# When the expert weights, the residual rows and the empty rows are loaded beside the attention of a cross-attention and mixture-of-experts kernel, and how far the weighted sums follow the scores

## What is computed

```
c = layernorm(x); q = ctx
s = (c*w_cq) @ q.T + (c @ w_c + b_c)[:, None] + (q @ w_q + b_q)[None, :] + b_cq
a = softmax(s, axis=1);  c2q = a @ q
b = softmax(max(s, axis=1));  q2c = b @ c
x = x + concat([c, c2q, c*c2q, c*q2c]) @ W_l.T + b_l
y = layernorm(x);  e = argmax(y @ wr + br)        # one of 8 experts per row
x = x + gelu(y @ w1[e] + b1[e]) @ w2[e] + b2[e]   # w1: 8 x 128 x 512, w2: 8 x 512 x 128
```

## Time and profile before

| what | us |
|---|---|
| median of 3 runs (lowest, highest) | 244.3 (244.2, 244.76) |
| the profiled execution | 246.33 |
| its span | 244.6 |
| TensorE busy | 199.7 (82%) |
| VectorE busy | 182.6 (75%) |
| ScalarE busy | 157.6 (64%) |
| GpSimd busy | 124.0 (51%) |
| DMA, hardware queue | 50.08 MB, 89.6% of 16 engines' span |

### The profile page before, as it was taken

The page is one execution under the profiler, slowest core; times in us unless marked ns, Lnnn a source line. Parts: engine busy times, 40 slices in busy tenths (PEclk is TensorE's granted clock), DMA queues, the critical chain, the costliest instruction groups (busy, mean ns, idle before and its releaser), DMA issues.

```text
span 244.6 us, 4979 instructions
## 1 busy us (share of the span) xinstructions
PE 199.7 (82%) x1833; PEld 149.1 (61%) x1833; DVE 182.6 (75%) x400; ACT 157.6 (64%) x248; POOL 124.0 (51%) x171
## 2 busy tenths in 40 slices
PE   0388849875749999999999999989995589799980
PEld 0133344652436776677676776769974479689960
DVE  2899865786229989899999799886886437577670
ACT  2732795684346996969979969689701437467640
POOL 3792414700597094299780997942400650016783
PEclk9999986999988999999999999999998579999995
DMA  6999998999999999999999999998950159999100
GB/s 225 381 200 232 221 214 189 198 247 244 225 219 240 209 268 272 203 226 205 242 197 271 230 208 219 194 233 185 191 123 3 65 202 345 325 382 365 47 22 0
DMA packets 141102, 51.78 MB, mean 212 GB/s; under 512 B 121108, under 2 KB 138917, under 8 KB 141078
## 3 DMA queue, kind: packets, MB, share of 16 engines
q1 hardware_dynamic: 140144, 50.08, 89.6%
q0 software_dynamic: 784, 1.38, 1.6%
q10 hardware_dynamic: 150, 0.00, 0.0%
HBM read 10.74 MB, written 3.75 MB: 59 GB/s over the span
## 4 chain that ended last, share of the span: by engine, by line
PE 36%; DMA 15%; SPq 13%; DVE 11%; issue 11%; POOL 7%; ACT 4%; POOLq 0%; DVEq 0%; ACTq 0%
SPq L383 9%; DMA PT<-Phl 7%; PE psX L1032 7%; PE psS L1016 5%; PE psS L1014 5%; PE psS L1015 5%; PE psO L1032 5%; POOL out_x L568 4%; DMA stageT<-in_ctxT 4%; PE psX L1034 4%; DVE Phl L782 3%; POOL rows_by_expert L562 3%; DMA S<-rows_by_expert 3%; PE psO L1034 2%; ACT S L618 2%
## 5 line engine op out<-in xcount | busy, mean ns | idle before, releaser
L765 DVE TENSOR_SCALAR_CACHE_REDUCE S<-psS 128x1024 f32<-128x1024 f32 x48 | 58.3, 1217 | 11.9 <-PE psS L1016 11.7
L618 ACT ACTIVATE S<-S,negb 128x1024 f32<-128x1024 f32 x48 | 55.0, 1145 | 15.5 <-DVE negb L773 15.5
L782 DVE TENSOR_TENSOR Phl<-S,Phl 128x1024 f16<-128x1024 f32 x39 | 51.7, 1325 | 15.3 <-ACT Phl L633 15.2
L633 ACT CAST Phl<-S 128x1024 f16<-128x1024 f32 x48 | 50.2, 1045 | 16.4 <-DMA PT<-Phl 15.1
L500 POOL TENSOR_TENSOR Phl<-S,Phl 128x256 f16<-128x256 f32 x36 | 23.5, 685 | 53.2 <-ACT Phl L633 53.2
L1032 PE MATMUL psO<-qn,PT 128*128 128x256 f16 x204 | 36.5, 273 | 6.6 <-DMA PT<-Phl 6.6
L1014 PE MATMUL psS<-qT,gh 128*128 128x512 f16 x96 | 38.3, 399 | 3.1 <-DVE gl L743 2.8
L1032 PE MATMUL psX<-qn,PT 128*128 128x256 f16 x204 | 37.6, 279 | 3.7 <-DMA PT<-Phl 3.7
L1015 PE MATMUL psS<-qT,gh 128*128 128x512 f16 x96 | 37.9, 395 | 0.0
L1016 PE MATMUL psS<-qT,gl 128*128 128x512 f16 x96 | 37.9, 395 | 0.0
L1034 PE MATMUL psX<-qn,PT 128*128 128x128 f16 x204 | 36.2, 223 | 0.0
(11 more groups left out here) (232 smaller groups left out, 421.6 us busy)
## 6 DMA issues: line engine op xcount, KB each, us to landing
PT<-wp SPq DMA_DIRECT2D x8, 512.0 KB, 7.4
stageT<-in_ctxT SPq DMA_DIRECT2D x6, 512.0 KB, 7.2
qn<-wp SPq DMA_DIRECT2D x6, 512.0 KB, 8.5
wp<-in_w SPq DMA_DIRECT2D x4, 512.0 KB, 4.8
stageT<-in_w SPq DMA_DIRECT2D x4, 512.0 KB, 4.7
rows_by_expert<-stageT SPq DMA_DIRECT2D x4, 385.5 KB, 4.3
S<-rows_by_expert SPq DMA_DIRECT2D x2, 514.0 KB, 7.5
S<-rows_by_expert SPq DMA_DIRECT2D x2, 385.5 KB, 7.1
```

Source lines behind the costliest of these rows:

```text
L618: nc.scalar.activation(slot(t, e), slot(t, e), ACT.Exp, bias=negb[:, t:t + 1], accum_out=Lp[:, t * NG + e:t * NG + e + 1]).then_inc(exp_do ...
L633: nc.scalar.copy(hi, slot(t, e)).then_inc(high_done, 1)
L765: nc.vector.tensor_scalar(out=into, in0=bank(u, n)[:, 0:into.shape[1]], scalar1=1.0 / GS, scalar2=None, op0=ALU.mult, op1=ALU.max, accum_o ...
L782: nc.vector.tensor_tensor(lo, slot(t, e), hi, ALU.subtract).then_inc(low_done, 1)
```

## The change

On SP: the qn transposes are issued in the order 0, 2, 1, 3, 5, 4, 6, with no load between them. Two w1 loads follow them, ahead of PT(0,0); the other two come behind PT(1,0) and PT(1,3). The w2 loads come behind PT(t,5) of tiles 1 to 4, x_re behind PT(2,2), and the five fills behind PT(7,6). On GpSimd: product, cast and gl of the late columns of c, the first two of which were ScalarE's. On ScalarE: the copies of cT come before the first exp. On TensorE: `turn_c(1)` ahead of S(0,6), `row_terms()` ahead of S(1,5), and W(0,0..3) behind S(1,3..6), W(0,4..6) behind S(2,0..2); from W(1,0) on as before. The rest of GpSimd's program is unchanged.

```diff
@@ -372,8 +372,7 @@
             sp.dma_start(wrs[:, :], wr).then_inc(late_landed, 16)
             sp.dma_start(wl[:, :, :], wlT.rearrange("(k p) o -> p k o", p=P)).then_inc(late_landed, 16)
 
-            k = E // H
-            for n in range(NG):
+            for n in (0, 2, 1, 3, 5, 4, 6):
                 sp.wait_ge(qTh_ready, n + 1)
                 if n in DVE_LOW:
                     sp.wait_ge(qTl_ready, DVE_LOW.index(n) + 1)
@@ -381,9 +380,6 @@
                     sp.wait_ge(qTl_pool_ready, POOL_LOW.index(n) + 1)
                 src, dst = rows_of(n)
                 sp.dma_start_transpose(dst, src).then_inc(qn_landed[n], 16)
-                if n < H:
-                    sp.dma_start(w1raw[:, n * WC:(n + 1) * WC].rearrange("p (e f) -> p e f", f=F),
-                                 w1[n * k:(n + 1) * k].rearrange("e h f -> h e f")).then_inc(w_landed[n], 16)
 
             def transpose(t, e):
 
@@ -393,31 +389,42 @@
                 src, _, _, dst = piece(t, e)
                 sp.dma_start_transpose(dst, src).then_inc(pT_landed[e], 16)
 
+            def load_w1(k):
+
+                n = E // H
+                sp.dma_start(w1raw[:, k * WC:(k + 1) * WC].rearrange("p (e f) -> p e f", f=F),
+                             w1[k * n:(k + 1) * n].rearrange("e h f -> h e f")).then_inc(w_landed[k], 16)
+
             def load_w2(k):
 
                 n = E // H
                 sp.dma_start(stageT[:, k * WC:(k + 1) * WC].rearrange("p (e k d) -> p e k d", k=FC, d=D),
                              w2[k * n:(k + 1) * n].rearrange("e (k p) d -> p e k d", p=P)).then_inc(w_landed[H + k], 16)
 
+            load_w1(0)
+            load_w1(1)
             transpose(0, 0)
             for r in (0, 32):
                 sp.dma_start(b12f[r:r + E, 0:F], b1).then_inc(b12_landed, 16)
                 sp.dma_start(b12f[r:r + E, F:F + D], b2).then_inc(b12_landed, 16)
             for e in range(1, NG):
                 transpose(0, e)
-                if e > 1 and e - 2 < H:
-                    load_w2(e - 2)
-            sp.dma_start(x_re, x.rearrange("(t p) d -> p t d", p=P)).then_inc(x_re_landed, 16)
 
             for t in range(1, T):
                 for e in range(NG):
                     transpose(t, e)
-                    if e == 5 and t <= FILLS:
-                        sp.wait_ge(empty_ready, 2)
-                        k0, k1 = (t - 1) * RING, min(t * RING, NB)
-                        sp.dma_start(xs[k0 * P:k1 * P, :].rearrange("(k p) w -> p k w", p=P),
-                                     empty[:, :].unsqueeze(1).broadcast_to([P, k1 - k0, ROW]))\
-                            .then_inc(slots_emptied, 16)
+                    if t == 1 and e in (0, 3):
+                        load_w1(2 + e // 3)
+                    if t == 2 and e == 2:
+                        sp.dma_start(x_re, x.rearrange("(t p) d -> p t d", p=P)).then_inc(x_re_landed, 16)
+                    if e == 5 and t <= H:
+                        load_w2(t - 1)
+
+            sp.wait_ge(empty_ready, 2)
+            for k in range(FILLS):
+                k0, k1 = k * RING, min((k + 1) * RING, NB)
+                sp.dma_start(xs[k0 * P:k1 * P, :].rearrange("(k p) w -> p k w", p=P),
+                             empty[:, :].unsqueeze(1).broadcast_to([P, k1 - k0, ROW])).then_inc(slots_emptied, 16)
 
             expert_reg = [sp.alloc_register(f"expert{j}") for j in range(NB)]
             sp.wait_ge(w_low, T)
@@ -500,6 +507,12 @@
                     last = nc.gpsimd.tensor_tensor(lo[:, r], slot(t, e)[:, r], hi[:, r], ALU.subtract)
                 last.then_inc(low_pool_done, 1)
 
+            pool.wait_ge(vecs16_ready, 1)
+            pool.wait_ge(cT_ready, 2)
+            nc.gpsimd.tensor_scalar(g32[:, CH:N], cT[:, CH:N], vecs16[:, 0:1], vecs16[:, 1:2], ALU.mult,
+                                    ALU.add).then_inc(late_g_ready, 1)
+            pool.wait_ge(late_g_ready, 1)
+            nc.gpsimd.tensor_copy(gh[:, CH:N], g32[:, CH:N]).then_inc(late_gh_ready, 1)
             pool.wait_ge(late_gh_ready, 1)
             nc.gpsimd.tensor_tensor(gl[:, CH:N], g32[:, CH:N], gh[:, CH:N], ALU.subtract).then_inc(late_gl_ready, 1)
             low_piece(0, 3)
@@ -593,23 +606,16 @@
                     act.wait_ge(consts_ready, 4)
                 nc.scalar.copy(columns(n)[0], stageT[:, a:b]).then_inc(qTh_ready, 1)
 
+            act.wait_ge(cT_in_psum, 1)
+            act.wait_ge(g_ready, 2)
+            nc.scalar.copy(cT[:, 0:CH], cT_psum[0][:, :]).then_inc(cT_ready, 1)
             deviation(2, H, T)
             act.wait_ge(shift_ready, 1)
             for t in range(H, T):
                 nc.scalar.activation(c_sb[:, t, :], x_sb[:, t, :], ACT.Identity, bias=sc1[:, t:t + 1],
                                      scale=rstd[:, t:t + 1]).then_inc(c_late_ready, 1)
-
-            def keep_columns():
-
-                act.wait_ge(cT_in_psum, 2)
-                act.wait_ge(g_ready, 2)
-                for h in range(2):
-                    nc.scalar.copy(cT[:, h * CH:(h + 1) * CH], cT_psum[h][:, :]).then_inc(cT_ready, 1)
-                act.wait_ge(vecs16_ready, 1)
-                nc.scalar.activation(g32[:, CH:N], cT_psum[1][:, :], ACT.Identity, bias=vecs16[:, 1:2],
-                                     scale=vecs16[:, 0:1]).then_inc(late_g_ready, 1)
-                act.wait_ge(late_g_ready, 1)
-                nc.scalar.copy(gh[:, CH:N], g32[:, CH:N]).then_inc(late_gh_ready, 1)
+            act.wait_ge(cT_in_psum, 2)
+            nc.scalar.copy(cT[:, CH:N], cT_psum[1][:, :]).then_inc(cT_ready, 1)
 
             def exp_piece(t, e):
 
@@ -636,8 +642,6 @@
                 for e in range(NG):
                     exp_piece(t, e)
                     high(t, e)
-                    if t == 0 and e == 1:
-                        keep_columns()
                     if t == T - 1 and e == 1:
 
                         act.wait_ge(nM_ready, 1)
@@ -1022,6 +1026,8 @@
                 pe.wait_ge(pT_landed[e], 16 * (t + 1))
                 if t == 0:
                     pe.wait_ge(qn_landed[e], 16)
+                if t == 0 and e == 0:
+                    pe.wait_ge(cT_ready, 1)
                 if t == 1 and e == 0:
                     pe.wait_ge(row_term_ready, 1)
                 if e == 0 and t > 1:
@@ -1038,7 +1044,6 @@
             def row_terms():
 
                 pe.wait_ge(cT_ready, 2)
-                pe.wait_ge(late_g_ready, 1)
                 nc.tensor.matmul(psX[:, 0:T], ones[0:3, :], b3r[:, :], start=True, stop=False, skip_group_check=True)
                 for t in range(T):
                     last = nc.tensor.matmul(psX[:, t:t + 1], cT[:, t * P:(t + 1) * P], vecs[:, 2:3],
@@ -1052,16 +1057,23 @@
                 elif c % 2 == 0:
                     pe.wait_ge(qTl_pool_ready, POOL_LOW.index(c // 2) + 1)
                 scores(0, c)
-            turn_c(1)
+                if c == NCH - 2:
+                    turn_c(1)
             for u in range(1, T):
                 if u == H:
                     pe.wait_ge(late_gl_ready, 1)
                 for n in range(NG):
-                    if u == 1 and n == 3:
+                    if u == 1 and n == 5:
                         row_terms()
                     for c in range(2 * n, min(2 * n + 2, NCH)):
                         scores(u, c)
-                    if n >= AHEAD:
+                    if u == 1:
+                        if n >= 3:
+                            weighted(0, n - 3)
+                    elif u == 2 and n < AHEAD:
+                        if n < 3:
+                            weighted(0, NG - 3 + n)
+                    elif n >= AHEAD:
                         weighted(u - 1, n - AHEAD)
                     elif u > 1:
                         weighted(u - 2, NG - AHEAD + n)
```

## The result

On one chip the changed kernel takes a median of 251.75 us (249.94 to 252.84, four runs), the kernel before 244.53 (244.2 to 245.59, four runs): a ratio of 1.028, 95% interval 1.0209 to 1.0351. The profiled execution took 252.84 us; its span is 251.1 against 244.6, the mean granted clock 0.922 against 0.947.

The account below looks back on a forecast made before the run. The middle was taken as TensorE-bound, the start as held by late transposes in SP's load-filled queue. S(4,1) 2.5 us late plus 2.0 of clock, fills 0, gave +4.5 on 244.3: 248.8 us, range 243 to 253.5.

Parts of the forecast that it names:

- Tile 0's transposes, the earlier sums.: Start: PT(0,0) lands at 36.5 instead of 42.9, but tile 1's maximum comes at 49.3, no earlier than before.
- The start's gain.: TensorE reaches W(1,0) at about 60 instead of 70.86, worth about 11 us if nothing else came.
- L: Landing time of the moved x_re load, forecast at 84.8 us, with a load among transposes priced at 2.7 us.
- GpSimd behind it.: After x_re lands, GpSimd's add, split(0) and low_piece(2,3) take 11.1 us, to 95.9; S(4,1) starts 2.5 late.
- The clock.: TensorE's half clock after standing about 12 us costs 2.0 us, taken between 1.7 and 3.1.
- "No further loss, at most 2 us": After the stall SP clears the waiting transposes and w2(1) as fast as TensorE takes them; at most 2 us lost.
- Fills.: Five fills behind PT(7,6) need 11.1 us under 11.4 of cover, just hidden; 4 us exposed at slowest landing.
- (1): Rival: the queue ahead of x_re is short, landing it at 77.8, result 242 us; chance 0.11.
- (3): Rival: more stall, transposes can't catch up, 3.1 us of clock and fills exposed, 252 to 256; chance 0.17.
- (2): Rival: GpSimd's wait for x_re does not reach the pieces, so full gain, 233 us; chance 0.04.
- (4): Rival: no change, 244 us, with loads near their lower bound alone; chance 0.04.
- (5): Rival: change differs from its words; w1(0), w1(1) still precede tile 0, spreading them gives 5.4 off PT(0,0); no share.

Follow-up runs that it names:

- e1: The changed kernel with only the x_re load put back in its old place behind PT(0,6): 238.02 us against 246.08, ratio 0.9679.
- e3: The kernel before with only the x_re load moved behind PT(2,2), GpSimd's program untouched: 255.69 us against 246.08, ratio 1.0367.
- e2: The changed kernel, x_re load left late, GpSimd's wait and add of b_l moved behind the last split: 244.26 us against 246.08, ratio 0.9882.
- e4: The changed kernel with the five fills put back into tiles 1 to 5: 255.82 us against 246.08, ratio 1.0382.
- e10: e1 with e9's placing of the w1 and w2 loads, tile 0's sums ten pieces behind as in the change: ratio 0.9661 to the kernel before.
- e11: The changed kernel with w2(1..3) moved later, behind PT(4,5), PT(5,0) and PT(5,3): ratio 1.0244 to the kernel before.
- e6: e1 with tile 0's weighted sums twelve pieces behind again, as in the kernel before: 234.79 us against 245.84, ratio 0.9575.
- e5: e1 with w1(2) and w1(3) moved behind PT(0,2) and PT(0,4): 235.28 us against 245.84, ratio 0.9579.
- e9: e6 with w1(2), w1(3) behind PT(1,5), PT(2,5) and w2 loads at (3,3), (4,3), (5,0), (5,5): ratio 0.960 to the kernel before.
- e12: e9 with the last two w2 loads moved to (5,1) and (6,0): ratio 0.9655 to the kernel before.
- e8: e5 and e6 together, loads spread and tile 0's sums twelve pieces behind: 236.63 us against 245.84, ratio 0.9652.

## Why the prediction was right

**The sign and the mechanism.** It was forecast that GpSimd, in its fixed order, would take low_piece(2,3) only behind x_re, and that SP, VectorE, ScalarE and TensorE would all end in that wait. The traces show each, and e1 and e3 show that it alone makes the change slower. The forecast of 248.8 is 4.5 us above before; measured are 7.2 by the medians (5.1 to 8.6 by the interval) and 6.5 by the spans, so it is 2 us or more short. 251.75 lies within the 243 to 253.5 of the prediction, but 0.25 above the band of 246 to 251.5 that held its main share of 0.64. Step by step:

- *Tile 0's transposes, the earlier sums.* W(0,0) at 36.5: measured 35.70. Tile 1's negb at 49.3: 50.33. The sum has a slip of 0.5 here: its terms add up to 46.6 and 49.8, not 46.1 and 49.3. PT(1,0) issued at 53.2: 54.38, 1.2 late with the negb. Six kernels are the same up to this negb (after, e1, e2, e4, e10, e11), and it starts between 47.81 (e1) and 50.18 (after): from 44 to 48 us the granted clock was 0.66 and 0.50 in after and 1.00 in e1. So a difference of 2 us at negb 1 between two single profiles means nothing by itself. "Tile 1's exponentials start no earlier" held, and e6 shows why it mattered: it is the new order that keeps them late.
- *The start's gain.* W(1,0) at about 60: 61.39, 9.5 us earlier than before and not 10.9. 11 us "if nothing else came": e1 has 8 by its ratio, 9.1 by its span. "1 to 2 for loads in tiles 1 and 2" was mis-sized: TensorE's four waits for transposes from 60 to 83 us in e1 are 4.0.
- *x_re.* L = 84.8: 86.87. Of the 2.1, 1.2 is PT(1,0)'s start and 0.9 the queue, on 31.6. The Trainium skill's price for a load (DMA: Bandwidth & Descriptors, Bandwidth; an estimate of 1.5 us from its figure for 1 MB, which was measured on loads issued from GpSimd) would have had x_re there at 80.0; the trace goes with rows 3.
- *GpSimd behind it.* L to the end of the low part 11.1: 8.86, since split(0) took 4.0 us and not 6.2. This error and the last cancel: 95.9 forecast, 95.73 measured; S(4,1) forecast at 97.1, started at 97.14; negb 3 forecast at 99.1, ended at 98.95. The instant was right by luck, out of two wrong terms. Why split(0) was short is told in the last section: VectorE stood meanwhile.
- *The clock.* 2.0 taken between 1.7 and 3.1. From S(4,1) to the full clock in S(4,2) the work took 5.53 us where it takes some 2.8: 2.7. This is the first failed term, +0.7. The wait there was 10.3 us, and 3.7 in the row that I went by the earlier trace rows.
- *"No further loss, at most 2 us" after the stall*: the second, +1.3. Tiles 4 and 5 took 17.1 and 17.2 us where they had taken 16.6 and 15.9 (tile 7 gave 0.75 back); ScalarE waited 1.5 and 1.3 us for transposes. The queue that had stood 12.5 us had its backlog and w2 loads to clear. Of the two it is the loads: e11, with the same stall and without the loads in tiles 2 and 3, has these tiles at 15.8 and 16.6. "w2 in place of fills: within the queue's spare" is the step that failed.
- *Fills.* "Just hidden": they landed within 6.0 us of their issue, so by 195.2, ahead of the scatter at 197.46. Right, though a landing took longer than any in the earlier trace rows.
- *Other moves.* Product, cast and gl of the late columns took 2.5 us against 2.6, ahead of a 5.6 us wait for ScalarE: no cost. Moving the fills out of tiles 1 to 5 was "no gain"; by the traces of e4 it is one beside weight loads.

**Rivals.** (1), a short queue ahead of x_re, would have needed L near 78. (3), a longer stall with 252 to 256, came closer than its share of 0.17 says: 251.75 is just under its low end, and two of its three causes are in the trace in part: the clock at 2.7, and transposes that can't catch up. The third, fills exposed, is not. (2), the full gain with no wait reaching the pieces, and (4), no change through cheap loads, fall with the trace of GpSimd. (5) says that with w1(0) and w1(1) spread as well nothing behind L would alter but 2 us; that was not run. (The "eight" and the "words" it names stand in no text here; in the diff W(0,e) is ten pieces behind.)

The best kernels measured are e5 and e6, near 0.958 of before, 235 us. Left open: the 1.8 us that e2 loses behind its scatter, whether the place of a load within its tile matters, and whether the old order of sums could pass 0.957 with the add kept clear of VectorE's low parts as well; e9 and e12 did not.

## What to carry to other kernels

A DMA moved later in one engine's queue moves every wait for it on every other engine, and an engine's work behind such a wait is late even where it has nothing to do with the data: before moving a load, list what stands behind each wait for it and move those waits too, or don't move it. A queue that carries the critical transfers has room for loads where its consumer is slow for another reason, here in tile 0 with the new order of sums (e5; with the old order, e8, it had not), and the loads that were moved from one full stretch to another here took their loss along. When several edits come as one, undo them singly: here one line hid a gain of 3% in the rest, and one part of that rest, the earlier sums, cost about 1% beside the change's own loads (e1 against e6) and nothing beside e5's. A wait moved out of the way lands somewhere too: e2's add fell on VectorE's low part.

## What the hardware did that I had not expected

GpSimd and VectorE slow each other, but only in some pairs. Of GpSimd's split, four casts take 1.43 us and four differences 2.55 while VectorE is idle (above), 2.43 and 3.73 before (first line below and the earlier trace rows). What VectorE did beside them tells why. Kernel before, VectorE beside the cast at 71.89 and the differences at 74.40:

```profile
71.89 2.43 POOL L532 CAST wp<-wp 128x256 f16<-128x256 f32 x4
...
71.97 1.40 DVE L782 TENSOR_TENSOR Phl<-S,Phl 128x1024 f16<-128x1024 f32 x1 [5.49 <-ACT Phl L633]
...
74.43 1.72 DVE L782 TENSOR_TENSOR Phl<-S,Phl 128x1024 f16<-128x1024 f32 x1
```

And kernel after, GpSimd just behind the stall:

```profile
95.67 1.44 POOL L545 CAST wp<-wp 128x256 f16<-128x256 f32 x4
97.19 3.64 POOL L549 TENSOR_TENSOR wp<-wp 128x256 f16<-128x256 f32 x4
```

The casts at 95.67 ran beside VectorE's copy of scores(3,5), 95.85 to 97.00, and were not slowed; the differences at 97.19 ran beside its low part, begun at 97.00, and took 1.1 us more. Beside a low part in the kernel before the casts took 1.0 more as well, and VectorE's low part itself 1.40 and 1.72 us, where it takes 1.22 alone. So a low part on VectorE and a cast or differences on GpSimd cost 1.1 to 1.7 us together, and the copy out of PSUM cost nothing. GpSimd's add of x_re costs VectorE more. In e2, e8, e9 and e12 a low part began while the add ran, and each time it ended 1.1 us behind the add's end, after 2.85, 2.29, 3.40 and 2.23 us: as if it had stood until the add was done. The Trainium skill (GPSIMD Engine Reference, Specifications) says as much: the two share their SBUF interfaces, with contention where VectorE's instruction has two SBUF inputs; the traces agree, and add the price.

TensorE's clock, at half after 10.3 us of waiting, stayed there for some 5.5 us of full work; the short waits of up to 2.0 us in e1 left it at 1.00 in the window from 60 to 80 us.
